# Inverse of the softmax sums and root of the first normalisation: begun by ScalarE with logarithm and exp, finished by one Newton step on VectorE

## Time and profile before

| | |
|---|---|
| runs | 1228.41, 1230.52, 1232.91 us |
| profiled execution | 1230.85 us, its span 1228.3 us |
| TensorE busy | 1148.1 us, 93% |
| VectorE busy | 979.9 us, 80% |
| ScalarE busy | 639.9 us, 52% |
| GpSimd busy | 361.2 us, 29% |
| mean granted TensorE clock | 0.986 of full speed |

### The profile page before, as it was taken

The page is one execution under the profiler, slowest core; times in us unless marked ns, Lnnn a source line. Parts: engine busy times, 40 slices in busy tenths (PEclk is TensorE's granted clock), DMA queues, the critical chain, the costliest instruction groups (busy, mean ns, idle before and its releaser), DMA issues.

```text
span 1228.3 us, 23590 instructions
## 1 busy us (share of the span) xinstructions
PE 1148.1 (93%) x7884; PEld 767.8 (63%) x7928; DVE 979.9 (80%) x2541; ACT 639.9 (52%) x1001; POOL 361.2 (29%) x540
## 2 busy tenths in 40 slices
PE   6989999999999999999999867999999999999998
PEld 6857776877776777787677545444444444444443
DVE  6868989989899998998998746666666678777776
ACT  5254354345335435434533433655556568777774
POOL 1135336345444534634644331000000012111111
PEclk9989999999999999999999969999999999999999
DMA  8554664565565466456555532455554211667772
GB/s 269 127 135 109 170 175 118 152 176 138 142 177 149 110 173 165 113 164 171 146 139 145 143 121 77 144 204 199 204 206 175 95 60 35 187 219 239 237 223 94
DMA packets 100522, 191.10 MB, mean 156 GB/s; under 512 B 13376, under 2 KB 30912, under 8 KB 100416
## 3 DMA queue, kind: packets, MB, share of 16 engines
q1 hardware_dynamic: 100416, 189.75, 52.4%
HBM read 89.16 MB, written 43.91 MB: 108 GB/s over the span
## 4 chain that ended last, share of the span: by engine, by line
DVE 37%; PE 35%; issue 24%; DMA 2%; ACT 1%; SPq 1%; POOL 0%; DVEq 0%; POOLq 0%
PE bank L858 18%; DVE bank L1192 7%; PE bank L521 4%; PE bank L522 4%; PE bank L523 4%; DVE bn L1138 3%; DVE roped L1218 3%; DVE rt L1215 2%; DVE rt L1216 2%; DVE row_max L1192 2%; PE bank L605 2%; DVE neg_max L1233 2%; DVE x_res L1185 2%; DVE nt_t L292 2%; DVE nt_t L291 1%
## 5 line engine op out<-in xcount | busy, mean ns | idle before, releaser
L1192 DVE CUSTOM_DVE_ANT_0 bank<-bank,mask 128x256 f32<-128x256 f32 x512 | 201.8, 454 | 43.5 <-PE bank L605 36.6
L858 PE MATMUL bank<-wout_int,g_lo 128*128 128x512 bf16 x512 | 193.6, 379 | 1.1
L819 PE MATMUL bank<-qT_lo,win_int 128*128 128x512 bf16 x496 | 188.0, 379 | 1.2
L858 PE MATMUL bank<-wout_int,g_hi 128*128 128x512 bf16 x491 | 185.8, 379 | 0.3 <-issue 0.2
L819 PE MATMUL bank<-qT_hi,win_int 128*128 128x512 bf16 x474 | 179.6, 379 | 0.0
L961 ACT ACTIVATE probs<-bank 128x512 f32<-128x512 f32 x256 | 143.2, 604 | 36.8 <-PE bank L639 32.2
L1529 POOL TENSOR_SCALAR_AFFINE_SELECT probs<-probs 128x256 f32<-128x256 f32 x256 | 108.6, 427 | 80.4 <-ACT probs L961 74.3
L605 PE MATMUL bank<-k_st,q_st 96*128 96x256 f32 x512 | 98.8, 305 | 25.1 <-DVE row_max L1192 23.3
L1484 DVE TENSOR_TENSOR g_lo<-h_int,g_hi 128x512 f16<-128x512 f32 x128 | 89.1, 696 | 41.4 <-ACT g_hi L1101 37.8
L1522 POOL TENSOR_TENSOR x_res<-x_res,wo_b 128x512 f32<-128x512 f32 x32 | 43.4, 1375 | 253.8 <-DMA x_res<-in_x 246.5
L1069 ACT ACTIVATE h_ring<-bank,b_in,g_scale 128x512 f32<-128x512 f32 x96 | 73.0, 778 | 71.3 <-PE bank L819 54.8
(11 more groups left out here) (170 smaller groups left out, 2725.5 us busy)
## 6 DMA issues: line engine op xcount, KB each, us to landing
hidden_scratch<-h_ring SPq DMA_DIRECT2D x96, 256.0 KB, 2.1
h_ring<-hidden_scratch SPq DMA_DIRECT2D x96, 256.0 KB, 2.8
k_st<-k_hi SPq DMA_DIRECT2D x128, 128.0 KB, 2.7
q_st<-q_hi SPq DMA_DIRECT2D x128, 128.0 KB, 2.6
xq<-x_scratch SPq DMA_DIRECT2D x16, 1024.0 KB, 5.9
x_ln<-in_x SPq DMA_DIRECT2D x16, 512.0 KB, 4.5
ctx_raw<-in_ctxT SPq DMA_DIRECT2D x16, 512.0 KB, 5.0
k_st<-k_lo SPq DMA_DIRECT2D x64, 128.0 KB, 2.7
```

Of the source, the lines that this page charges most:

```text
L819: mm = pe.matmul(bank[f % 4][:], win_int[:, c, f * P:(f + 1) * P], part[:, par, c], start=c == 0 and part is qT_hi, stop=c == KC - 1 and p ...
L858: return pe.matmul(bank[4 * par + u][:], part[:, f % 4, u * P:(u + 1) * P], wout_int[:, f], start=f == 0 and part is g_hi, stop=f == FC - ...
L1192: dve.tensor_tensor_reduce(sc, sc, mask[:, (1 - qb) * P:(1 - qb) * P + S], 1.0, NEG, ALU.add, ALU.max, row_max[:, qb, n:n + 1]).then_inc(m ...
```

## The change

- `invert(b)`: ScalarE computes ln of the sums into `den_r` and then exp of minus that (`inv_start`, placed between `norm1` and `xt_lead`). VectorE makes one Newton step of two instructions on 128 x 256, with the sums read from PSUM, in place of RECIPROCAL.
- `ln1` is split. `ln1_stats` (moments and variance plus eps, 5 instructions) moves ahead of `quantise_win`. ScalarE's `root1` computes ln and exp(-0.5 ln) on 128 x 2 after head 10's exp. `ln1_finish` makes one Newton round and `nmr`, 4 instructions, after `quantise_win`. The two guessing operations and two Newton rounds are gone.
- The second transpose of x goes into `bank[6]`, the first bank of the v and probability products; it waits for a copy out of that bank in the step before and no longer for `den_done`. `v_tile(j, 0)` now waits for `xt_lo`, and the second q tile waits for `den_done`.
- ScalarE's `ctx_hi(b + 2)` moves from behind head 9's exp to ahead of the copies of the maxima. `oT_copy(b, 0)` and `centre(b - 1, 0)` move from between the exps of heads 12 to 14 to behind the last exp.
- GpSimd's four `ctx_lo(b + 2, c)` move from behind bands 10 to 13: two ahead of band 0, one behind band 1, one behind band 3.
- One activation table set is asked for at the start by name.

The last inverse, after step 15, is as before.

```diff
-LN1_OPS = 17
+LN1_OPS = 9
+LN1_STATS = 5
+        x_bank = [bank[4], bank[6]]
...
@@ x_transposes
+                elif j == 1:
+                    pe.wait_ge(v_done, 1)
                 else:
-                    wait(pe, den_done, j - 1)
+                    wait(pe, oT_out, 2 * j - 3)
...
-                    mm = pe.transpose(q_bank[s][:, c * P:(c + 1) * P], x_ln[:, s, c * P:(c + 1) * P], ident[:])
+                    mm = pe.transpose(x_bank[s][:, c * P:(c + 1) * P], x_ln[:, s, c * P:(c + 1) * P], ident[:])
@@ v_tile
+                if s == 0:
+                    pe.wait_ge(xt_lo, 2 * j + 2)
@@ qk_tile, q, half 1
+                else:
+                    wait(pe, den_done, j - 1)
@@ ScalarE
+            def root1(j):
+                act.wait_ge(ln1_chain, LN1_OPS * j + LN1_STATS)
+                act.activation(nt_t[:], veps[:], ACT.Ln).then_inc(ln1_root, 1)
+                act.wait_ge(ln1_root, 2 * j + 1)
+                act.activation(rstd[:], nt_t[:], ACT.Exp, scale=-0.5).then_inc(ln1_root, 1)
+
+            def inv_start(j):
+                act.wait_ge(den_mm, NC4 * (j + 1))
+                act.activation(den_r, den_bank[:, 0:S], ACT.Ln).then_inc(inv_root, 1)
+                act.wait_ge(inv_root, 2 * j + 1)
+                act.activation(den_r, den_r, ACT.Exp, scale=-1.0).then_inc(inv_root, 1)
...
+            act.preload_act_table_set("natural_log_exp_and_others")
+            root1(0)
...
@@ ScalarE, step
+                if has_o:
+                    inv_start(b - 1)
...
+                if has_xt:
+                    ctx_hi(b + 2)
                 max_copy(b, 0, slice(0, 2))
...
-                    if n == 9 and has_xt:
-                        ctx_hi(b + 2)
+                    if n == 10 and has_xt:
+                        root1(b + 2)
...
-                    if n == 12:
-                        oT_copy(b, 0)
-                    if n == 13 and has_o:
-                        centre(b - 1, 0)
+                oT_copy(b, 0)
                 if has_o:
+                    centre(b - 1, 0)
                     centre(b - 1, 1)
@@ VectorE, invert
-                dve.wait_ge(den_mm, NC4 * (b + 1))
-                dve.reciprocal(den_r, den_bank[:, 0:S]).then_inc(den_done, 1)
+                tmp = rt[:, 0, 0]
+                dve.wait_ge(inv_root, 2 * (b + 1))
+                wait(dve, dmax_done, 2 * b)
+                dve.scalar_tensor_tensor(out=tmp, in0=den_bank[:, 0:S], scalar=-1.0, in1=den_r,
+                                         op0=ALU.mult, op1=ALU.mult).then_inc(inv_step, 1)
+                dve.wait_ge(inv_step, b + 1)
+                dve.scalar_tensor_tensor(out=den_r, in0=tmp, scalar=2.0, in1=den_r,
+                                         op0=ALU.add, op1=ALU.mult).then_inc(den_done, 1)
@@ VectorE, step
+                if has_xt:
+                    ln1_stats(b + 2)
                 quantise_win(b)
                 if has_xt:
-                    ln1(b + 2)
+                    ln1_finish(b + 2)
@@ GpSimd, step
+                if has_xt:
+                    ctx_lo(b + 2, 0)
+                    ctx_lo(b + 2, 1)
                 for n in range(H):
                     band(b, n)
...
-                    if 10 <= n < 14 and has_xt:
-                        ctx_lo(b + 2, n - 10)
+                    if n in (1, 3) and has_xt:
+                        ctx_lo(b + 2, n // 2 + 2)
```

More of the change, by code:

```diff
@@ L204, in build @@
         ctx_in, xln_in, xres_in, win_in, x1_out = (sem(n) for n in ("ctx_in", "xln_in", "xres_in", "win_in", "x1_out"))
-        ln1_chain, ln1_norm = sem("ln1_chain"), sem("ln1_norm")
+        inv_root, inv_step = sem("inv_root"), sem("inv_step")
+        ln1_chain, ln1_root, ln1_norm = sem("ln1_chain"), sem("ln1_root"), sem("ln1_norm")
         ln2_chain, y2_done, dmax_done = sem("ln2_chain"), sem("y2_done"), sem("dmax_done")
@@ L286, in rsqrt_seed, with rsqrt @@
             link(dve.tensor_scalar(r.bitcast(I32), r.bitcast(I32), -1.0, RSQRT_SEED, ALU.mult, ALU.add))
-        def rsqrt(dve, link, v, r, tmp):
-            for _ in range(3):
+        def rsqrt(dve, link, v, r, tmp, rounds=3):
+            for _ in range(rounds):
                 link(dve.tensor_tensor(tmp, r, r, ALU.mult))
@@ L924, in xt_lead @@
                 act.wait_ge(xt_mm, 2 * j + s + 1)
-                lead(q_bank, s, xt_hi)
+                lead(x_bank, s, xt_hi)
             def oT_copy(j, half):
@@ L995, in _ @@
             ctx_hi(1)
+            root1(1)
             def step(b, par, has_c, has_o, has_proj, has_xt):
@@ L1140, in moments, with ln1_stats @@
                 link(dve.bn_aggr(mv[:, which, s], bn[:, which, s]))
-            def ln1(j):
+            def ln1_stats(j):
                 dve.wait_ge(xln_in, 16 * (j + 1))
@@ L1146, in ln1, with ln1_finish @@
                 moments(link, x_ln, 0, 1)
+                link(dve.tensor_scalar(veps[:], mv[:, 0, :, 1], EPS, None, ALU.add))
+                assert link.count[0] == LN1_STATS
+            def ln1_finish(j):
+                dve.wait_ge(ln1_root, 2 * (j + 1))
                 wait(dve, ln1_norm, 2 * j)
-                link(dve.tensor_scalar(veps[:], mv[:, 0, :, 1], EPS, None, ALU.add))
-                rsqrt_seed(dve, link, veps[:], rstd[:])
-                rsqrt(dve, link, veps[:], rstd[:], nt_t[:])
+                link = chain(dve, ln1_chain, LN1_OPS * j + LN1_STATS)
+                rsqrt(dve, link, veps[:], rstd[:], nt_t[:], 1)
                 link(dve.scalar_tensor_tensor(out=nmr[:], in0=mv[:, 0, :, 0], scalar=-1.0, in1=rstd[:],
                                               op0=ALU.mult, op1=ALU.mult))
-                assert link.count[0] == LN1_OPS
+                assert link.count[0] == LN1_OPS - LN1_STATS
             def ln2_moments(j, s):
@@ L1228, in xt_rest @@
             def xt_rest(j, s):
-                rest(q_bank, s, xt_hi, 2 * j + s + 1, xt_lo)
+                rest(x_bank, s, xt_hi, 2 * j + s + 1, xt_lo)
             def invert(b):
-                dve.wait_ge(den_mm, NC4 * (b + 1))
-                dve.reciprocal(den_r, den_bank[:, 0:S]).then_inc(den_done, 1)
+                tmp = rt[:, 0, 0]
[6 more added lines that the diff above has]
+                                         op0=ALU.add, op1=ALU.mult).then_inc(den_done, 1)
             def normalise(b, half):
@@ L1256, in _ @@
             dve.memset(idle_b, 0.0).then_inc(idle_done, 1)
-            ln1(0)
+            ln1_stats(0)
+            ln1_finish(0)
             dve.memset(neg_max[:], 0.0).then_inc(const_done, 1)
@@ L1299, in _ @@
             dve.wait_ge(c_in, 16 * TABLES)
-            ln1(1)
+            ln1_stats(1)
+            ln1_finish(1)
             weight_lo(4, "wo")
```

## The result

The changed kernel took 1246.99 us (median of 4, 1244.97 to 1248.62) against 1231.1 us of the kernel before on the same chip: ratio 1.013, 95% interval 1.0106 to 1.0155. The forecast was 1208.0 us, faster. It is 1.3% slower. The profiled execution's span is 1245.7 us.

The account below looks back on a forecast made before the run. TensorE and VectorE, both nearly full in attention, were taken as the bound. Period 43.87 to 42.3 us over 13 steps gives 20.4 us, with the rest 22.8: 1230.85 - 22.8 = 1208.0 us, range 1199 to 1219.

Parts of the forecast that it names:

- Two ctx_lo of 0.73 us fall ahead of band 0 into its idle time: GpSimd from M (start of split_max): two moved pieces fit its idle time; q_lo at worst 0.2 us later.
- 1.11 us at the last clump: Back half: TensorE's last clump waits 1.11 us for GpSimd's bands; forecast to go in full.
- The 0.52 us ahead of the second transpose: Front half, TensorE: the second transpose's wait for the RECIPROCAL, 0.52 us, forecast gone by using the other bank.
- M + 11.9 comes from exps 6 to 9, which TensorE paces: Start of SyncE's queue, at q_lo, 11.9 us after M: nothing in the change shortens the share's path from there.
- the share binds harder: Rival, chance 0.20: q_lo or the share's landing 0.7 us later, period 43.0 us, 1217 us in total.
- SyncE's chain is not lengthened: The argument set against the rival of a harder-binding share, which allowed for 0.7 us.
- Of the 3.5 us only the 1.0 of lateness can be worth anything: VectorE, back half: 3.5 us of small instructions go, but only its 1.0 us lateness at the turn can count.
- the back half: M to S (start of the next scores): 18.67 less the last clump's 1.11 gives 17.56 us.
- the front half: S (start of the next scores) to M (start of split_max): between 24.09 and 24.72 us, from 25.36.
- Maxima at S + 0.7: Sign at the turn: VectorE begins its maxima 0.7 us after the scores start, with TensorE as releaser.
- the rival of a slower kernel: Rival, chance 0.05: Ln and Exp lie in different tables, each pair loads twice; 1257 us at 2.0 us per load.
- The share next in line: Ahead of normalise: the share lands at M + 37.2, allowing a period of 42.0 to 42.2 us on average.

Follow-up runs that it names:

- b4: The kernel before with only the moves of ctx_hi, oT_copy, centre and ctx_lo, old ln1 and RECIPROCAL kept: 1246.04 us.
- a1: The changed kernel with one more wait: GpSimd starts the first two ctx_lo only after split_max: 1224.09 us.
- c1: The changed kernel with the moves of ctx_hi, oT_copy, centre and ctx_lo undone, the new arithmetic and other bank kept: 1221.94 us.
- a2: The changed kernel with 12 idle products on TensorE ahead of the transposes of the maxima: 1237.97 us.
- b1: a1 with idle products on TensorE, 6 ahead of head 14's scores and 3 ahead of the transposes of the maxima: 1216.22 us.
- a3: The changed kernel with spread_shares ahead of load_xres in SyncE's queue: 1249.75 us.
- c2: The kernel before with the moves and all three cures of b3, but RECIPROCAL and the old ln1: 1209.65 us.
- b3: a1 with b1's idle products and the write of the sums issued ahead of SyncE's wait for the store of x1: 1205.92 us.

## Why the prediction was wrong

**The step that failed first: "Two ctx_lo of 0.73 us fall ahead of band 0 into its idle time".** It was true of GpSimd and wrong for VectorE. I asked who waits for GpSimd, and not what runs beside it. Beside it runs split_max, on which transposes, copies and exps hang. The two instructions grew from 0.37 to 1.44 us, and the transposes start at M + 1.52 for M + 0.46. b4 shows that the moves without the arithmetic turn the kernel slow, a1 that one wait on GpSimd takes the 1.07 us back, and 22.9 us in all with the clock time that went with it. The Trainium skill (SBUF — State Buffer, SBUF: two separate sides) says that VectorE and GpSimd share a pair of ports as an exclusive lock, and that the one that starts first shuts the other out for its whole instruction. By the Trainium skill this holds for a VectorE operation in a two-port mode, and for one with two SBUF inputs when GpSimd's operation reads SBUF. The trace agrees in that each stretched instruction ends some 0.05 us behind one of GpSimd's two of 0.7 us. Which starts first it doesn't resolve: GpSimd's is recorded within 0.02 us behind M in eleven of the steps 1 to 13, and in one of these, step 4, M's instruction kept its 0.18 us. The sign was in my own rows: veps took 0.41 us for two columns, nmr 0.16.

**The term that was missing: TensorE's clock.** The sum had none. The moves took idle time of TensorE away from where it did no harm (1.11 us at the last clump), and it came up where VectorE holds TensorE next, the last 5 us ahead of M and the 1.5 behind it. The 0.52 us ahead of the second transpose did not do this: c1 has lost them too, and its gaps around M are those of before. Before, these gaps were mostly 0.26, 0.27 and 0.39 us, and the clock was full in all 14 steps; with 0.71, 0.27 and 0.38 (a1) it fell. The size: the forecast was 42.3 a step, measured 45.62, 3.3 over. The clock time lost is 30.6 us over 13 steps, 2.35, and the stretched split_max 1.0 on average; together 3.3. That the two add up so well is partly luck, since some of the loss lies under waits. That idle products alone took 9 us off (a2) and cut the low steps from 10 to 3 (b1) shows the clock as a cause, not as a sign.

**"M + 11.9 comes from exps 6 to 9, which TensorE paces".** Right, and I didn't follow it: when TensorE is slower behind M, all of it shifts. The copies of q started at M + 14.6 and the read of the share at M + 36.3 on average over steps 1 to 13, for 11.9 and 33.4. Of the rivals "the share binds harder" had the right place, but not the size (it allowed for 0.7 us) nor the cause: "SyncE's chain is not lengthened" overlooked that its start could move. a3 shows that an earlier share alone wins nothing.

**The bound by VectorE.** "Of the 3.5 us only the 1.0 of lateness can be worth anything" was still too much. c2 has the old arithmetic, but only 0.4 us of that lateness, since the small instructions shrink by themselves once GpSimd's work is not beside them, and its period equals b3's. The arithmetic is worth 9 us in the schedule of before (c1), nothing beside the uncured moves (b4), and in the cured schedule some 2 to 4 us, more than half of it ahead of step 0; the intervals of b3 and c2 overlap, so that this last figure is not clear of the noise.

**What held.** In b3, with full clock in steps 1 to 14, the back half is 17.5 us (17.9 in two steps; 17.56 forecast) and the front half 24.4 to 25.3, 24.9 on average, a little over its forecast of 24.1 to 24.7. Maxima at S + 0.7, with TensorE as their releaser. Ln and exp ended at S + 2.5 and the inverse at S + 3.4 (3.3 forecast), hidden. Two table loads, so the rival of a slower kernel had the wrong mechanism. The share next in line, at the point where it was put: all of its slack was gone, and normalise waited in ten of 13 steps. Step 0 to M was earlier by 3.9 us for 0.9; kernels with the old arithmetic have M of step 0 at 62.5 to 64.5, with the new at 60.3 to 62.4, so that about 2 us are the change's, and the rest is no more than kernels with the same arithmetic differ among themselves.

**Open.** What exactly makes the clock fall is not settled by these runs: with nearly the same three gaps it held in one step and fell in another (a1: held with 0.85, 0.26 and 0.39 us, fell with 0.71, 0.27 and 0.38). No run separates the moves on ScalarE from those on GpSimd in the kernel before. Whether a3 would have helped with GpSimd's queue in another order wasn't tried by itself.

## What to carry to other kernels

When an edit frees one engine of waits, write down where its idle time goes, not only that it goes: on TensorE, pieces that gather in a few microseconds can cost the clock, and the slow stretch then delays everything that is anchored in it. When work moves to an idle engine's free time, look at what runs beside it on engines that share its ports, above all at small instructions on the chain. And undo the moves and the arithmetic of a combined edit separately: here one part was worth 9 us and the other cost 15, and together they cost 16, so neither number holds beside the other part.

## What the runs showed of the hardware

- Six idle products of 128x256 (0.83 us) ahead of head 14 and three (0.50 us) ahead of the transposes, useless by themselves, kept the granted clock full in 11 of 14 steps (b1), for 4 of 14 without them (a1), where it fell three times with three gaps of 1.4 us together, and held once with 1.5.
- GpSimd's subtraction of 128x256 lengthened a 128x32 VectorE instruction from 0.18 to 0.78 us, and one of two columns from 0.16 to 0.3 to 0.7 us, while instructions of VectorE with a PSUM operand kept their time (x_res out of a bank and x_res, 128x512: 0.69 us beside GpSimd's subtractions and without them).
- In steps with a low clock the loss was 2.8 us of clock time each in the changed kernel and 3.1 in b4, and 1.7 where the gap behind M was short (a1) or filled (a2).
- Logarithm or exp of 128x2 took 0.20 us on ScalarE, of 128x256 0.38 from PSUM and 0.42 from SBUF; two dependent ones are 0.05 us apart or less.
